# Pooling tokens two batches at a time and running four experts side by side in the last phase of a single-core hybrid kernel

## The reference, cut to what matters

```python
logits = jnp.einsum('bsd,ed->bse', x, gate_w) + gate_b          # 32 experts
probs = jax.nn.softmax(logits, axis=1)                          # over the 1024 tokens
vals, idx = jax.lax.top_k(probs.transpose(0, 2, 1), K)          # each expert takes 8 tokens
...
pooled = jnp.einsum('bked,bke->bed', gathered, topv)            # 16 x 32 x 64
h = jnp.concatenate([pooled.transpose(1, 0, 2), ones], axis=-1)
h = jax.nn.gelu(jnp.einsum('ebd,edh->ebh', h, weight1), approximate=False)   # 65 -> 256
h = jnp.concatenate([h, ones], axis=-1)
out = jnp.einsum('ebh,eho->ebo', h, weight2)                    # 257 -> 64
...
outputs = outputs.at[jnp.arange(Bn)[:, None], flat_idx].add(weighted)
```

## Time and profile before

| | us |
|---|---|
| time, median of 3 runs | 6785.05 |
| lowest of them | 6782.85 |
| span of the profiled execution | 6778.7 |
| expert phase, first load issued to the end of the span (6611.6 to 6778.7) | 167.1 |
| TensorE busy over the span | 6279.5 |
| VectorE busy over the span | 6198.5 |

### The profile page before, as it was taken

One profiled execution on the slowest core, in us unless ns is written; L12 is line 12 of the kernel. 1 busy time (PEld: TensorE's weight loads), 2 busy tenths in 40 slices (PEclk: granted clock), 3 DMA queues, 4 the chain that ended last, 5 costly groups with the idle time before them and its releaser, 6 DMA issues. The chain is left out here.

```text
span 6778.7 us, 154979 instructions
## 1 busy us (share of the span) xinstructions
PE 6279.5 (93%) x52177; PEld 3795.6 (56%) x52177; DVE 6198.5 (91%) x3824; ACT 4532.8 (67%) x9559; POOL 2334.7 (34%) x6840
## 2 busy tenths in 40 slices
PE   8999989999969999999999999999999999999867
PEld 3567843333236666666666666666666666666535
DVE  7888878888849999999999999999999999999972
ACT  7888858888736666666666666666666666666641
POOL 5555545555423232332323323323233232332210
PEclk9999999999979999999999999999999999999995
DMA  6666666666622121121212212212122121221164
GB/s 143 155 154 154 155 145 153 156 153 156 153 68 54 39 63 47 48 54 47 55 47 48 56 44 58 50 42 59 47 52 51 42 59 47 51 49 42 27 187 115
DMA packets 929532, 563.47 MB, mean 83 GB/s; under 512 B 697101, under 2 KB 834221, under 8 KB 928941
## 3 DMA queue, kind: packets, MB, share of 16 engines
q1 hardware_dynamic: 928957, 556.40, 34.6%
HBM read 159.23 MB, written 124.13 MB: 42 GB/s over the span
## 5 line engine op out<-in xcount | busy, mean ns | idle before, releaser
L1029 DVE TENSOR_TENSOR_SCAN states<-decay,enter_ps 128x1024 f32<-128x1024 f32 x2048 | 4465.4, 2262 | 75.4 <-PE enter_ps L732 66.0
L857 ACT ACTIVATE decay<-rate_ps 128x512 f32<-128x512 f32 (+1 forms) x4096 | 2221.2, 594 | 338.0 <-PE rate_ps L718 146.0
L732 PE MATMUL enter_ps<-s_steps,s_tokens 128*128 128x128 bf16 x16384 | 2142.2, 310 | 293.5 <-DVE states L1029 284.1
L732 PEld LDWEIGHTS enter_ps<-s_steps,s_tokens 128*128 128x128 bf16 x16384 | 1596.5, 129 | 1415.3 <-DVE states L1029 1167.2
L718 PE MATMUL rate_ps<-s_wide,s_decays 128*128 128x256 bf16 x8192 | 1318.4, 283 | 14.2 <-ACT decay L857 7.6
L964 POOL TENSOR_TENSOR product<-decay,states 128x16 f32<-128x16 f32 x1920 | 462.2, 241 | 2195.2 <-ACT decay L857 2191.7
L243 POOL TENSOR_TENSOR entered<-gates 128x512 f32<-128x512 f32 x512 | 899.9, 1758 | 888.7 <-ACT gates L203 888.7
L864 ACT COPY enter_ps<-at_first 128x16 f32<-128x16 f32 x1920 | 338.1, 176 | 1223.9 <-PE enter_ps L732 1186.2
L760 PE MATMUL y_ps<-states,spread 128*32 128x512 f32 x8192 | 1090.3, 604 | 2.4 <-issue 2.4
L718 PEld LDWEIGHTS rate_ps<-s_wide,s_decays 128*128 128x128 bf16 x8192 | 904.3, 118 | 74.7 <-ACT decay L857 19.7
L161 PE MATMUL pre<-rows,weights_left 128*32 128x512 f32 x8192 | 905.4, 595 | 36.0 <-POOL rows L236 23.8
(11 more groups left out here) (135 smaller groups left out, 2473.3 us busy)
## 6 DMA issues: line engine op xcount, KB each, us to landing
rows<-feat SPq DMA_DIRECT2D x1024, 132.0 KB, 2.4
rows<-feat SPq DMA_DIRECT2D x512, 128.0 KB, 2.4
s_steps<-steps_dram SPq DMA_DIRECT2D x4096, 8.0 KB
rows<-feat SPq DMA_DIRECT2D x512, 127.8 KB, 2.4
s_wide<-rates_dram SPq DMA_DIRECT2D x1024, 32.0 KB, 1.9
s_tokens<-tokens_dram SPq DMA_DIRECT2D x2048, 16.0 KB, 2.0
rates_dram<-parts SPq DMA_DIRECT2D x64, 384.0 KB, 3.3
steps_dram<-parts SPq DMA_DIRECT2D x64, 384.0 KB, 3.4
```

Source lines behind the costliest of these rows:

```text
L732: mm = pe.matmul(out.rearrange("p h l -> p l h"), tokens[s][:, k, :], steps[s][:, k, :, d:d + half], start=True, stop=True)
L857: act.activation(decay[i][:, half, at:], rate_ps[h][:, :, at:], ACT.Exp).then_inc(decay_ready, 1)
L1029: dve.tensor_tensor_scan(out, factor, term, 0.0, ALU.mult, ALU.add).then_inc(scanned, 1)
```

## The change

**Loads.** All four logit tiles and all eight token tiles get buffers of their own, so that no load waits for a buffer. A token tile now holds two batches (a *duo*, 128 partitions). The queue's order becomes: logits 0, identity, logits 1, duos 0 and 1, logits 2, duos 2 and 3, logits 3, duos 4 to 7, then `w1`, `w2` in one transfer with pieces of 128 values instead of 64, the bias row, and the residual.

**Pooling.** Transposes are 128 x 128, eight for a duo. Eight matmuls for a duo take 128 weight columns (both batches) and 64 moving columns (both batches' choices); half of the 128 x 64 result is of use, and DVE copies the two 64 x 32 blocks on the diagonal. `chosen_t` has two buffers.

**First layer.** The roles are swapped: `pooled` of an expert is the weight (65 x 32, batches 16 to 31 are zeros) and `w1` of the expert is moving, 256 columns. Experts 4m to 4m + 3 write partitions 0, 32, 64 and 96. Four banks of 128 x 512 pass through Gelu.

**Between the layers.** 16 transposes of `hidden` (128 x 128) and four DVE copies are new. `hidden` is read with a step of two values.

**Second layer.** 96 matmuls as before, now with 32 weight columns and again four experts beside each other in the partitions of one bank. One DVE copy of 128 x 512 replaces four of 16 x 512; four transfers store the results instead of one.

```diff
+            load_logits(0)
             sp.dma_start(ident[:, :], identity).then_inc(consts_in, DMA)
-            def load_tokens(b):
-                if b >= 2:
-                    sp.wait_ge(normed_turned, b - 1)
-                sp.dma_start(normed[b % 2][:, :], normed_dram[b, :, :]).then_inc(normed_in[b % 2], DMA)
...
+            for q in range(2, QUADS):
+                load_logits(q)
+                load_tokens(2 * q - 2)
+                load_tokens(2 * q - 1)
+            for j in range(2 * QUADS - 2, DUOS):
+                load_tokens(j)
             sp.dma_start(w1[:, :, :], weight1.rearrange("e d h -> d e h")).then_inc(weights_in, DMA)
-            for h in range(2):
-                sp.dma_start(w2[:, h, :, :], weight2[:, 128 * h:128 * h + 128, :].rearrange("e h o -> h e o")
-                             ).then_inc(weights_in, DMA)
+            sp.dma_start(w2[:, :, :, :].rearrange("p e h o -> p e (h o)"), weight2[:, 0:HIDDEN, :].rearrange(
+                "e (p h) o -> p e (h o)", h=HALVES)).then_inc(weights_in, DMA)
...
-            sp.dma_start(expert_dram, results[:, :, :]).then_inc(results_out, DMA)
+            for j in range(LANES):
+                dst = expert_dram.rearrange("b (m j) o -> j b m o", j=LANES)[j, :, :, :]
+                sp.dma_start(dst, results[ROW * j:ROW * j + BATCH, :, :]).then_inc(results_out, DMA)
...
+            def pool_tokens(j):
+                q, first = 2 * j // GROUP, 2 * j % GROUP
+                pe.wait_ge(chosen_t_ready, 2 * (q + 1))
+                pe.wait_ge(normed_t_ready, 2 * (j + 1))
+                if j >= 2:
+                    pe.wait_ge(pooled_ready, j - 1)
                 for t in range(TILES):
+                    mm = pe.matmul(pooled_ps[j % 2][:, 0:2 * EXPERTS], normed_t[j % 2][:, t, :],
+                                   chosen_t[q % 2][:, t, EXPERTS * first:EXPERTS * first + 2 * EXPERTS],
+                                   start=(t == 0), stop=(t == TILES - 1))
...
-            for e in range(EXPERTS):
-                for h in range(2):
-                    at = (e % 16 * 2 + h) * BATCH
-                    mm = pe.matmul(work_ps[:, e // 16, at:at + BATCH], w1[:, e, 128 * h:128 * h + 128],
-                                   pooled[:, :, e], start=True, stop=True)
...
+            def first_layer(k):
+                for m in (2 * k, 2 * k + 1):
+                    for j in range(LANES):
+                        e, at = LANES * m + j, HIDDEN * (m % 2)
+                        mm = pe.matmul(hidden_ps[k][ROW * j:ROW * j + ROW, at:at + HIDDEN], pooled[:, e, :],
+                                       w1[:, e, :], start=True, stop=True)
+                mm.then_inc(hidden_summed, 1)
...
+            def second_layer(k):
+                pe.wait_ge(hidden_t_ready, k + 1)
+                for m in (2 * k, 2 * k + 1):
+                    for h in range(HALVES + 1):
+                        for j in range(LANES):
+                            e = LANES * m + j
+                            out = results_ps[ROW * j:ROW * j + ROW, CH * m:CH * m + CH]
+                            if h < HALVES:
+                                mm = pe.matmul(out, hidden_t[:, m, h, ROW * j:ROW * j + ROW], w2[:, e, h, :],
+                                               start=(h == 0), stop=False)
+                            else:
+                                mm = pe.matmul(out, ones[:, :], w2_bias[:, e, :], start=False, stop=True)
+                return mm
...
+            for k in range(4):
+                first_layer(k)
+            turn_hidden(0)
+            turn_hidden(1)
+            second_layer(0)
+            turn_hidden(2)
+            second_layer(1)
...
+            def move_pooled(j):
+                dve.wait_ge(pooled_summed, j + 1)
+                for i in range(2):
+                    p = dve.tensor_copy(pooled[0:CH, :, 2 * j + i],
+                                        pooled_ps[j % 2][CH * i:CH * i + CH, EXPERTS * i:EXPERTS * i + EXPERTS])
+                p.then_inc(pooled_ready, 1)
```

203 lines of the change are left out of this document (103 added, 100 removed).

## The result

The changed kernel takes 6695.95 us (median of 4 runs, 6694.86 to 6702.31), beside 6785.24 for the kernel before. The ratio is 0.9873, with a 95% interval from 0.9858 to 0.9887. One of the four runs of the kernel before took 18169.33 us; the other three lie between 6782.85 and 6785.42.

What follows compares the result with a forecast made beforehand. The prediction took the phase to be bound by transfers until 6645, then by TensorE at 1.2 GHz, then a tail. Its terms, -21.7 - 38.8 + 1.5 = -59.0 us, gave a span of 6719.7 and a time of 6726 us, range 6702 to 6745.

Steps and rivals of the forecast that it cites:

- The way to the first layer: First load to first layer: token wait gone, pooling priced at the low clock, first layer starting at 6675.5, 21.7 us less.
- by the weight columns alone: Pooling record price: old pooling (0.119 us) and first-layer (0.215) records differ only there, so 0.215 for the new one.
- The width itself is worth almost nothing: Pooling: 128 records at 0.215 us against 256 at 0.119, 27.5 us against 30.4; the gain is the wait.
- The layers: First layer to results: 5.1 + 4.0 + 1.0 + 6.9 = 17.0 us against 55.8, 38.8 us less.
- about 5 us shorter together: Transposes between the layers and second layer, priced at 1.2 GHz: what both would save at 2.4 GHz.
- the estimate of 9.6 us for 192 records: Second layer: issue at 60 cycles per matmul at 1.2 GHz, which would put 4.5 us on the sum.
- The tail: After the results: three more store issues at about 0.43 us and smaller pieces, 1.5 us more.
- The full clock comes already during pooling: Rival: TensorE gets 2.4 GHz from about 6630, the weights' landing bounds the first layer's start; 6704 us, chance 0.14.
- a pooling record doesn't add its two sides: Denies the rival that weight load and moving side don't overlap in pooling: 42.2 us instead of 27.5; 6741 us, chance 0.07.
- the experts overlap: Denies the rival that packed experts run one behind the other in both layers: 38 us more, 6764 us, chance 0.07.
- The rival of late weights: TensorE waits for weights ahead of the first layer, below 167 GB/s; at 150 the start slips by 8, 6734 us; chance 0.04.
- Same at 0.98: Whole kernel: chance that the time lies within 2% of 6785 us (6649 to 6921); faster 0.01, slower 0.01.

Runs made afterwards that it cites:

- run with narrow records: The changed kernel with each pooling record of 64 moving columns split into two of 32, transposes and weights still 128 wide; 6741.97 us.
- pooling alone: The kernel before with only the pooling of duos new, the weights still loaded ahead of duo 1 and the layers as before; 6758.40 us.
- run with the layers alone: The kernel before with the packed first and second layer and four stores, a buffer for every load and tokens loaded by duos; 6744.63 us.
- kernel with blocks side by side: The changed kernel with each 128 x 64 pooling record replaced by two of 64 x 32 in different halves of TensorE's columns; 6705.05 us.
- the version that puts all together: The changed kernel with gap-filling matmuls, 64 x 32 pooling blocks, `w1` in two loads, quad 0 chosen earlier, result stores and loads on two queues; 6693.52 us.
- the filled one: The changed kernel with 15 extra matmuls of 128 x 512, results unread, in TensorE's waits at the start and for the results; 6696.41 us.

## Why the prediction was wrong, point by point

**The way to the first layer: -42.2 us (85.6 to 43.4), forecast -21.7.** The failed step is the clock. The prediction priced all pooling records at 0.215 us, the price at 1.2 GHz, and gave the full clock during pooling a chance of 0.14, with the argument that "47 us busy of 52 in pooling and 55 of 56 behind it stayed at 0.50". That row is right, but it was measured on records of other shapes (64 weight columns with 32 moving ones, and 128 with 16), and it was carried over to records with 128 and 64. What the runs showed in its place: the new pooling brings the full clock within its first quad (at 6637.7), and its 128 records cost 17.1 us, not 27.5. The run with narrow records shows that the argument holds for those, busy 47.8 us of 48, clock 0.57. What it is in the wider records that brings the clock stays open, since two records of 64 x 32 side by side bring it too. The rest of this part came out near. The record costs 0.219 us at 1.2 GHz, the wait for tokens is gone, the last tokens had landed 21.6 us behind the first load (forecast 19) and the weights 40.8 (forecast 42), both by the landings in the trace. The price of the record was right, its reason wasn't shown: the two rows it compares differ in the moving columns and the rows too, and not "by the weight columns alone". With the clock, pooling ended 42.8 us behind the first load instead of 63.3.

**The worth of the width.** "The width itself is worth almost nothing" is right for the cost of a record at one clock (0.219 for what two records at 0.119 did), and wrong for the kernel: pooling alone brings 27 us, most of it by the clock that the wider record brings (3.6 us of the way to the first layer came by buffers and duos in the run with the layers alone). It is the clearest case of the mistake, a price per record taken as if the record had no effect on the clock at which it is priced.

**The layers: -44.3 us (55.8 to 11.5), forecast -38.8.** Packing was priced well. At the low clock the layers take 18.8 us, against 18.7 from the terms. The change got 11.5 where the forecast was 17.0, since the clock was up from the start; "about 5 us shorter together" was the term left out. Of the single terms, the second layer took 7.7 us where the sum had 6.9, and 1.0 us left for gaps was not needed. Inside the second layer two errors partly cancel: at the low clock sixteen records take 0.59 us, 0.037 each, where the sum had 0.107 / 4 = 0.027, while a group of eight bias records with its changes takes 0.37 where the sum gives 0.44. The Trainium skill's TensorEngine Tiling (Array Packing), section Instruction Overhead, has about 60 cycles for each matmul. The rows come near it: 0.037 us at 1.2 GHz are 44 cycles, and 0.36 us for sixteen at 2.4 GHz are 54 each. So the estimate of 9.6 us for 192 records at the low clock, from the Trainium skill's figure, was too high by a third (192 x 0.037 = 7.1), and mine of 5.1 too low by over a quarter. Its advice not to take the tiling factor from a dimension that is already small was no reason against packing here: the factor was taken from the 16 weight columns, and even at this price the layer went from 27.6 us (27.59 busy) to 7.7 at the same clock, with 4.0 of new transposes. The moving side was 64 columns before and after, and no run here makes it smaller.

**The tail: +3.1 us, forecast +1.5.** Four stores of the results are issued in 2.56 us where one took 0.32, 0.60 each instead of the 0.43 taken from the loads behind them, and the way from the copy to the final matmuls takes 8.05 us instead of 6.40. And the final matmuls take 17.01 us where they took 15.56, because the clock, low at their start in both kernels, came back 6 us into them instead of 3.

**The sum of the phase.** Forecast 108.1 us, measured 83.7: 20.5 less on the way to the first layer, 5.5 less in the layers, 1.6 more in the tail. In the profiled executions that is the whole error but for the later start of the phase, 4.8 us: the span came out 19.5 us below its forecast. The other 10.6 us of the 30 lie between the medians and the profiled executions: the prediction added 6.35 us to the span, and the median of the changed kernel lies 4.2 us below its span, since its slowest run was profiled. The first load was issued at 6611.62 in the profile of before and between 6610.98 and 6619.48 in those of the other kernels, with the same code ahead of it.

**The rivals.** "The full clock comes already during pooling" is what happened: the work of pooling shrank with the clock. In one thing it was told wrong: not the weights' landing bound the first layer's start in the changed kernel (they had landed 2.6 us earlier) but pooling itself, whose last copy by VectorE releases the layer. Its time, 6704, was 8 us too high, 3.5 of them because it took 2 us for what the full clock saves in the layers (5.5), and 1.5 by a slip in its sum (6726 - 21.5 - 2 is 6702.5); in the profiles its phase of 86 us stands against 83.7 and 81.4. The others did not happen: a pooling record doesn't add its two sides, the experts overlap, and the weights weren't late in the changed kernel. (The rival of late weights moved the start by 8 us at 150 GB/s; its own numbers give 7.) The weights were late, by 4.3 and 2.2 us, in two variants whose pooling ended somewhat earlier, so the limit was close. The Trainium skill, TensorE: Matmul & The Clock Gate, section Why this matters for your kernels, lets continuous busy time bring the clock. The prediction noted that the old pooling spoke against it, and the narrow records speak against it again. It could have drawn the other conclusion from that, namely that something else than being busy decides, and that a change of the records might alter just this.

**The chances.** Same at 0.98 was right. The range was too narrow at the low end: a rival with a chance of 0.14 sat at its edge, and its own error of 8 us was not in the range. A two-level clock makes two separate forecasts, and the second deserved its own bounds.

## What to carry to other kernels

The price of a TensorE record and the clock at which it runs are not independent: when a change alters the shape of the records in a long stretch, forecast the clock anew, and don't take the level from the old shape, however busy the old stretch was. Ask of every wait at the full clock what runs behind it: in the kernel with blocks side by side a wait of 4.3 us for a transfer was followed by a first layer of 7.02 us instead of 3.66, so that faster pooling ahead of the transfer gained nothing. And the order of issue belongs to packing: the same 96 matmuls of the second layer, expert by expert, took 13 us more in the profile, while the first layer didn't mind.

## What the runs showed of the hardware that was not expected

- Back-to-back records with 128 weight columns and 32 moving ones held the granted clock at 0.57 over 48 us with TensorE busy 47.8; the same weights with 64 moving columns had it at 1.00 from 8.7 us behind the first work on `chosen`. With 128 weight and 16 moving columns a clock of 1.00 was lost 2.9 us into the old first layer behind the new pooling, with no gap in it. Two 64 x 32 records side by side brought it in two kernels (at 6629.0 and at 6642.3).
- The clock was also lost in short waits: in one of 2.07 us with 1.19 us idle shortly before (the version that puts all together), and at the end of one of 4.26 us (blocks side by side). It was kept through one of 1.26 us in the changed kernel and one of 1.85 us in the filled one.
- At the full clock sixteen records of 64 moving columns, four side by side, take 0.36 us, 0.0225 each.
- Loads in one queue ran at 417 GB/s for the tokens (128 partitions, 4096-byte pieces), 180 for `w1` (65 partitions, 1024-byte pieces) and 259 for `w2` (128 partitions, packets of 2048 bytes). The rate of `w1` was 191 in another execution of the same kernel.
- The start of a phase varied by 8.5 us between executions of the same code ahead of it, so that stretches must be compared from a common event, not from the start of the span.
